# A graph attention layer on one core: the first stage rewritten, from the loading of x to the first row of weights

## The reference

```python
h = maximum(layernorm(x), 0.0)              # eps 1e-5
Wh = h @ W_w + W_b
e = leaky_relu((Wh @ a1)[:, None] + (Wh @ a2)[None, :], negative_slope=0.2)
attention = softmax(where(adj > 0, e, -9e15), axis=1)
out = x + attention @ Wh
```

## Time and profile before

| | us |
|---|---|
| median of 3 runs (lowest, highest) | 1554.79 (1554.2, 1555.71) |
| the profiled execution, its whole time | 1553.04 |
| the profiled execution, span from first to last instruction | 1551.1 |
| busy: PE, DVE, ACT, POOL | 1448.3, 1425.4, 1110.9, 593.7 |

### The profile page before, as it was taken

The page is one execution under the profiler, slowest core; times in us unless marked ns, Lnnn a source line. Parts: engine busy times, 40 slices in busy tenths (PEclk is TensorE's granted clock), DMA queues, the critical chain, the costliest instruction groups (busy, mean ns, idle before and its releaser), DMA issues.

```text
span 1551.1 us, 30326 instructions
## 1 busy us (share of the span) xinstructions
PE 1448.3 (93%) x12740; PEld 1258.0 (81%) x12740; DVE 1425.4 (92%) x1155; ACT 1110.9 (72%) x975; POOL 593.7 (38%) x1096
## 2 busy tenths in 40 slices
PE   2880899979999999999999999999999999999998
PEld 2760787768888888888888888888888888888887
DVE  4654999999999999999999999999999999999994
ACT  3664788877777677768777777768777777767771
POOL 0866433334444344334434343434343434423000
PEclk9995899999999999999999999999999999999999
DMA  9719866668776777778777877778767877676000
GB/s 195 80 14 118 65 44 48 44 60 103 56 55 59 100 56 52 52 84 81 52 52 63 100 54 53 60 99 57 54 49 62 103 55 53 49 97 50 1 1 28
DMA packets 170768, 99.07 MB, mean 64 GB/s; under 512 B 19472, under 2 KB 167568, under 8 KB 170640
## 3 DMA queue, kind: packets, MB, share of 16 engines
q0 software_dynamic: 147456, 67.17, 61.2%
q1 hardware_dynamic: 23184, 30.05, 7.1%
HBM read 290.06 MB, written 8.42 MB: 192 GB/s over the span
## 4 chain that ended last, share of the span: by engine, by line
PE 82%; DVE 12%; issue 2%; DMA 2%; ACT 1%; SPq 0%; DVEq 0%; POOL 0%; ACTq 0%; POOLq 0%
PE acc L636 77%; DVE work L515 4%; PE acc L612 3%; DVE work L508 3%; DVE X L521 1%; DMA work<-in_x 1%; PE acc L604 1%; DMA q_rows<-q_j 1%; DVE adj_cols L457 1%; DVE xr L408 1%; ACT work L323 1%; PE acc L647 0%; DMA work<-q_rows 0%; DVE xr L414 0%; ACT work L338 0%
## 5 line engine op out<-in xcount | busy, mean ns | idle before, releaser
L636 PE MATMUL acc<-X,work 128*128 128x257 f16 x12288 | 1372.6, 273 | 12.9 <-DVE work L515 12.9
L636 PEld LDWEIGHTS acc<-X,work 128*128 128x128 f16 x12288 | 1189.4, 97 | 188.8 <-DVE work L515 16.8
L251 POOL DMA_DIRECT2D adj_rows<-in_adj x1024 | 550.8, 545 | 776.0 <-DVE adj_cols L457 752.5
L338 ACT ACTIVATE work<-work 128x2048 f16<-128x2048 f32 x256 | 487.6, 1907 | 276.7 <-PE acc L636 274.0
L508 DVE SCALAR_TENSOR_TENSOR work<-work,sigma,adj_cols 128x2048 f32<-128x2048 f32 x256 | 594.6, 2323 | 20.8 <-issue 17.3
L515 DVE SCALAR_TENSOR_TENSOR work<-work 128x2048 f16<-128x2048 f32 x256 | 584.9, 2285 | 29.3 <-ACT work L338 29.2
L323 ACT ACTIVATE work<-work,r_j 128x1024 f32<-128x1024 f32 x256 | 278.1, 1134 | 28.3 <-DMA work<-q_rows 17.9
L323 ACT ACTIVATE work<-q_odd,r_j 128x1024 f32<-128x1024 f32 x256 | 278.5, 1135 | 23.3 <-DVE work L515 23.3
L457 DVE STREAM_TRANSPOSE adj_cols<-adj_rows 128x512 int32<-128x512 int32 x256 | 176.0, 699 | 0.0
L612 PE MATMUL acc<-q_odd,xr 128*128 128x258 f32 x256 | 68.8, 393 | 9.0 <-DVE X L426 9.0
L647 PE MATMUL acc<-mean_wh,tiny 128*128 128x257 f16 x64 | 17.7, 276 | 47.1 <-DVE work L515 46.5
(11 more groups left out here) (60 smaller groups left out, 54.0 us busy)
## 6 DMA issues: line engine op xcount, KB each, us to landing
adj_rows<-in_adj POOLq DMA_DIRECT2D x1024, 64.0 KB, 3.7
work<-in_x SPq DMA_DIRECT2D x16, 512.0 KB, 21.4
xr<-in_x SPq DMA_DIRECT2D x16, 512.0 KB, 4.0
out<-xr SPq DMA_DIRECT2D x16, 512.0 KB, 3.8
work<-q_rows SPq DMA_DIRECT2D x4, 512.0 KB, 5.7
q_odd<-q_rows SPq DMA_DIRECT2D x4, 512.0 KB, 5.4
q_odd<-in_L_gnn_W_w SPq DMA_DIRECT2D x2, 128.0 KB, 2.1
xr<-in_L_gnn_a SPq DMA_DIRECT2D x2, 128.0 KB, 6.1
```

What stands on the lines that cost most here:

```text
L251: pool.dma_start(rows8[QP * q:QP * (q + 1), n % R8], adj_v[s, m, k, q]).then_inc(s_rows[n % R8], 16)
L338: nc.scalar.mul(Et[:, at:at + 2, 0, :], Wt[:, i % RING], SCALE).then_inc(s_H, 1)
L636: return nc.tensor.matmul(acc[:, m, 0:F1], Et[:, 2 * (k % RING) + e, 1 if n == 2 else 0, m * P:(m + 1) * P], X16[:, 2 * k + e, 1 if n == 1 ...
```

## The change

- **x in seven groups** of 4, 4, 8, 8, 8, 16 and 16 blocks. The first group is issued ahead of W. The bias is no longer waited for at the start.
- **Norm factors on VectorE alone**: the inverse root by three Newton steps from a guess made from the exponent (in place of ACT's square root). The statistics of later groups are spread over the pairs by a table, so that all of them lie in pairs 0 to 18 of 32.
- **Blocks in pairs.** ACT normalises in place in x; POOL sums h in place of Wh. ACT copies the transposed even blocks, VectorE the odd ones. Six banks of PSUM hold h W (without bias), and the f16 parts of c_j h_j W are made straight from there: c_j is a factor of the pair's own t (`column_exps`, `greater_t`, `scale_columns`), so it needs no extremes. `x_high` on ACT and `x_low` on VectorE thus lie in the pair loop and no longer in the first super row; L426's addition is gone. r_j and sigma take up the pair's factor: sigma has a column for each unit.
- **Bias**: the softmax weights sum to one, so W_b is added to the rows of x that the output needs, by an accumulating DMA from POOL once per half super row.
- **Extremes over partitions** by a matmul against the identity, a maximum, and a matmul that spreads the two values.
- **q**: the eighth of q that the first super row needs is stored by a DMA of its own and loaded at once; the other stores follow. POOL holds further adjacency loads until it is there. The first 8 sets of adjacency are issued quadrant by quadrant between the additions.
- **First super row**: the first unit is multiplied alone, and ACT makes its upper part after two products in place of four.

```diff
+    GROUPS = [(0, 0, 1, 0), (0, 1, 2, 4), (0, 2, 4, 8), (1, 0, 2, Y), (1, 2, 4, Y + 8), (2, 0, 4, 2 * Y), (3, 0, 4, 3 * Y)]
+    STATS_AT = [None, None, (0, 2), (2, 2), (5, 2), (8, 4), (14, 4)]
...
             sp.wait_ge(s_qn, 1)
-            for q in range(NQ):
-                sp.dma_start(q_store[q], q_j[QP * q:QP * (q + 1), :].rearrange("p (z e) -> p z e", e=4)).then_inc(s_qst, 16)
+            store_q(0, 0, NZ // 2, s_q0)
+            sp.wait_ge(s_q0, 16)
+            load_q(0)
+            store_q(0, NZ // 2, NZ, s_qst)
+            for q in range(1, NQ):
+                store_q(q, 0, NZ, s_qst)
             sp.wait_ge(s_qst, 16 * NQ)
-            load_q(0)
+            sp.wait_ge(s_X, NB)
...
+            def add_bias(s, half):
+                pool.wait_ge(s_xr[half], 16 * s + 16)
+                pool.dma_start(xr[:, half], W_b.rearrange("(o m f) -> o m f", o=1, m=1).broadcast_to([P, H, F]),
+                               accum_op=ALU.add).then_inc(s_xb[half], 16)
+
+            for b in range(1, NB):
+                add_h(b)
+                if EARLY <= b < EARLY + NQ * SETS:
+                    load_quadrant(*divmod(b - EARLY, NQ))
+            pool.wait_ge(s_q, 16)
             for n in range(SETS, NSET * NS):
                 load_adj(n)
+                if n % NSET == 2 * R8 + 3:
+                    for half in range(2):
+                        add_bias(n // NSET, half)
...
+            for p in range(PAIRS + 1):
+                if p >= 2:
+                    x_high(2 * p - 4)
+                    x_high(2 * p - 3)
+                if 2 * p + 3 < NB:
+                    normalise(2 * p + 3)
+                if p >= 1:
+                    column_exps(p - 1)
+                if 2 * p + 2 < NB:
+                    copy_hT(2 * p + 2)
+                if 2 * p + 4 < NB:
+                    normalise(2 * p + 4)
...
+            def pair(p):
+
+                copy_hT(2 * p + 1)
+                if p >= 1:
+                    read_s_t(p - 1)
+                norms(p, 0)
+                if p >= 1:
+                    greater_t(p - 1)
+                norms(p, 1)
+                if p >= 2:
+                    x_low(2 * p - 4)
+                norms(p, 2)
+                if p >= 2:
+                    x_low(2 * p - 3)
+                norms(p, 3)
+                if p >= 1:
+                    scale_columns(p - 1)
...
-            def unit_low(g, i):
-                if g < NC:
-                    x_low(NI * g + i)
-                low(g, i)
...
+            def project(b):
+                k = b % 2
+                pe.wait_ge(s_hT[k], b // 2 + 1)
+                if b >= WH:
+                    pe.wait_ge(s_X, b - WH + 1)
```

More of the change, by code:

```diff
@@ L284, in copy_hT @@
+            def copy_hT(b):
                 act.wait_ge(s_ht, b + 1)
-                if not first:
+                if b >= 2:
                     act.wait_ge(s_whp, b - 1)
-                nc.scalar.copy(hT[:, k, :], ps_hT[k][:, 0:F]).then_inc(s_hT, 1)
-            normalise(0, 0, True)
-            normalise(1, 1, True)
-            copy_hT(0, 0, True)
-            normalise(2, 0, False)
-            copy_hT(1, 1, True)
-            def pairs(lo, hi):
-                with act.Fori(lo, hi) as pair:
-                    for k in range(2):
-                        normalise(2 * pair + k + 1, (k + 1) % 2, False)
-                        copy_hT(2 * pair + k, k, False)
@@ L301, in _ @@
[L301 to L312 removed]
+                nc.scalar.copy(hT[:, 0, :], ps_hT[0][:, 0:F]).then_inc(s_hT[0], 1)
@@ new lines, in _ @@
+            for p in range(PAIRS):
+                pair(p)
+                if p == 0:
+                    bounds()
+                if p >= PAIRS - TURNED:
+                    transpose(0, p - PAIRS + TURNED)
+            read_s_t(PAIRS - 1)
+            dve.wait_ge(s_st, PAIRS)
+            t_in = s_t[:, :, 1]
+            nc.vector.tensor_reduce(ext[:, 0:1], t_in, AX.X, ALU.max)
+            step(nc.vector.tensor_reduce(sc[:, 4:5], t_in, AX.X, ALU.min))
+            nc.vector.tensor_scalar(ext[:, 1:2], sc[:, 4:5], -1.0, None, ALU.mult).then_inc(s_ext, 1)
@@ L625, in _ @@
-            transpose_h(NB - 1, 1, False)
-            project(NB - 2, 0, False)
-            project(NB - 1, 1, False)
-            pe.wait_ge(s_sum, NB)
-            for k in range(2):
-                ins = nc.tensor.matmul(ps_tot[:, 0:F], ones, wh_sum[:, k, :], start=(k == 0), stop=(k == 1))
+            transpose_h(0)
+            transpose_h(1)
+            pe.wait_ge(s_wa, KF)
+            project(0)
+            transpose_h(2)
+            project(1)
+            pe.wait_ge(s_ones, 1)
+            pe.wait_ge(s_bound, 1)
@@ new lines, in _ @@
+            nc.tensor.matmul(ps_sum, ones, sc[:, 16:17], start=True, stop=True).then_inc(s_sq, 1)
+            for b in range(2, NB - 1):
+                transpose_h(b + 1)
+                if b == 5:
+                    pe.wait_ge(s_sqr, 1)
+                project(b)
+            project(NB - 1)
+            pe.wait_ge(s_ext, 1)
+            nc.tensor.matmul(ps_top[0:2, 0:P], ext[:, :], ident, start=True, stop=True).then_inc(s_extT, 1)
+            pe.wait_ge(s_dg, 1)
+            nc.tensor.matmul(ps_top[:, P:P + 2], ones[0:2, :], sc[0:2, 22:24], start=True, stop=True).then_inc(s_top, 1)
@@ L631, in _ @@
+            pe.wait_ge(s_hsum, NB - 1)
+            pe.wait_ge(s_X, NB - 3)
+            for c in range(KF):
+                ins = nc.tensor.matmul(ps_hb[:, c * P:(c + 1) * P], h_sum[:, c * P:(c + 1) * P], ones, start=True, stop=True)
+            ins.then_inc(s_col, 1)
+            pe.wait_ge(s_hb, 1)
+            for c in range(KF):
+                ins = nc.tensor.matmul(ps_mean[:, 0:F], hb[:, c * P:(c + 1) * P], Wx[:, c, 0:F], start=(c == 0), stop=(c == 1))
             ins.then_inc(s_tot, 1)
```

527 lines of the change are left out of this document (292 added, 235 removed).

## The result

The changed kernel takes **1511.35 us** (median of 4 runs, 1510.69 to 1512.79); the kernel before, run beside it, 1555.1 us. The ratio is 0.9718, with a 95% interval of 0.9704 to 0.9732: 43.8 us faster, where the prediction said 28.5 (1526.6). The time lies outside the central forecast (1519 to 1533) and 0.35 us inside the lower end of the wide range (1511 to 1546). That it is still inside is luck: one of the four runs, 1510.69, is not. So the direction and the course of the time line held, and the size was 15 us off. The profiled run took 1511.28 us with a span of 1509.5.

A forecast was written before the change was run, and what follows sets the result against it. VectorE was taken to bound the first row, and only time before 350.0 us could move. That row ending 28.2 us earlier gave a span of 1522.9; plus 1.94 and 1.75, 1526.6 us (central 1519 to 1533, wide 1511 to 1546).

The forecast's parts named there:

- Start: Before the pair loop: with x's first 4 blocks issued first, the loop starts at about 17 us instead of 27.
- Pairs 0 to 18: First part of the pair loop, bound by VectorE: its work and waits sum to 77 us, ending at 94 us.
- rival (a): VectorE's small steps in pairs 0 to 18 are cheaper and miss POOL's additions: 62 us there, 1511 in all; chance 0.15.
- port waits: In pairs 0 to 18, POOL's additions hold up small VectorE operations: 4 us over the pairs, 5 in five chains.
- Pairs 19 to 31: Rest of the pair loop: ACT sets the pace at 2.4 us a pair, 31 us, ending at 125 us.
- Rival (b): Something new (TensorE's clock in pairs 0 to 18, q, or adjacency) is late by 6 to 20 us; chance 0.23.
- Extremes: After the pair loop: two tiny matmuls and small steps replace POOL's 5.90 us; 5.5 to 6 us to q, at 131.
- q: q's way through DRAM before the first unit: store 3.0 us, load 4.4, back at 138.5 us.
- First unit: After q is back: products, weights and low part let TensorE start 9.1 us later, at 147.6 us.
- First row: TensorE becomes the bound, VectorE next by 0.29 us a unit; cold clock costs 3.4; 174.2 us, ending at 321.8.
- Edits that cost nothing: The bias by accumulating DMA from POOL after the row's 28th set, and sigma per pair, add no time.
- From span to median: Outside the kernel's span: 1.94 us around it, plus 1.75 by which the runs' median exceeded the profiled run.

The follow-up runs named there:

- the last kernel: The changed kernel with POOL's pause, copies of pairs 0 to 18 on ScalarE, four filled chain pairs and 48 extra matmuls before the first unit: 1503.76 us.

## Why the prediction was right in direction and short in size

**What bounds the kernel** was read rightly: only the time before 350.0 us moved. **Start**: 16.46 us for 17.

**Pairs 0 to 18** is the mis-sized term, 77 forecast and 69.66 measured. A statistics pair on VectorE (start, duration, what):

```profile
54.33 0.42 DVE L476 COPY xr<-acc 128x256 f32<-128x256 f32 x1
54.66 0.15 DVE L481 COPY xr<-acc 128x4 f32<-128x4 f32 x1
54.73 1.39 DVE L438 BATCH_NORM_STATS2 xr<-work 128x6 f32<-128x256 f32 x4
56.05 0.19 DVE L486 TENSOR_SCALAR xr<-xr 128x1 f32<-128x1 f32 x1
56.16 0.86 DVE L496 SCALAR_TENSOR_TENSOR X<-acc,c_j,X 128x256 f16<-128x256 f32 x2
56.94 0.21 DVE L492 TENSOR_SCALAR c_j<-c_j,sc 128x2 f32<-128x2 f32 x1
57.07 0.41 DVE L476 COPY xr<-acc 128x256 f32<-128x256 f32 x1
```

From start to start the copy takes 0.33 us, the read of s and t 0.07, the greater t 0.11, the two low parts 0.78 and the factors 0.13: 1.42 us instead of 1.78. The three small operations make 0.29 of the difference, the copy and the low parts the rest. I had priced the three at 0.2 each, the spacing of two that wait for one another; here none reads what the one ahead wrote, and each shows 0.15 to 0.21 us of duration but takes 0.07 to 0.13 of the engine's time. The difference of 0.36 in 19 pairs is 6.8 us. The port waits were 9 in the sum, 4 in the pairs and 5 in the chains; leaving the additions out shortens the chain pairs by 3.8 us and the whole stretch by 4.2 to 4.6, so about 4.6 was too much. Together 11.4 too much. Against it stand 3.2 us that I did not have, VectorE's waits up to pair 19 for TensorE's transposes (1.7), for the bound on W (1.1) and for an exponential (0.4). In one place the two overlap: 0.7 us of wait for transposes in pair 13 is also gone without the additions. So 0.9 to 1.6 us is left that I did not follow. The chains themselves were sized rightly: their dependent operations come 0.20 to 0.21 apart (62.54 to 62.75).

The mechanism of rival (a) is thus what happened in this term, with half of its 15 us; that its total, 1511, is also the measured one is luck, the sum of six smaller misses of the same sign.

**Pairs 19 to 31**: TensorE binds them, with 2.19 us a pair once the clock is up, not ScalarE with 2.4; the three pairs at reduced clock gave 1.25 us of that back.

**Rival (b), the clock.** The prediction named a clock at 0.5 within the loop as a sign that it would be wrong. The clock did fall there, to 0.67 on average between 28.8 and 38.5 us, 0.79 between 49 and 57, 0.66 between 65 and 70 and 0.72 between 86 and 92, behind the gaps of the chain pairs. The Trainium skill's page that the prediction cited for this rival (TensorE: Matmul & The Clock Gate) describes such an alternation, and the trace agrees that it occurs; what the rival had wrong is the price. It said 5 to 15 us; the kernel with filled gaps puts it at about 1.2 us in pairs 19 to 21 and 0.8 in pair 13, and at nothing that shows in the statistics pairs, because VectorE, not TensorE, is late there. The price is that of this kernel: with the copies on ScalarE, up to 4.4 us of VectorE's waits hang on the half clock. The row that I used against the rival did not bear on this loop. The length of a single gap does not tell the two apart: the loop before idled for 3.02 us up to 45.05 and 3.17 up to 66.00 and its clock stayed at 1.00, while the changed one idled for 1.73 and 1.31 us in pairs 12 and 13 and fell to 0.50 at 66 us. What decides is open. One more reading was loose: the block of 2.15 us (30.17 to 32.32) was taken as one at half clock, though the granted clock of that stretch is given as 1.00. The figure itself holds, since a block of the changed kernel takes 2.15 us too (31.50 to 33.65), at a granted clock of 0.50.

**Extremes**: 4.97 for 5.8. The parts that the prediction lists add up to 5.3, not 5.8; of the rest, the two dots and their sum took 1.0 us instead of 1.5 (116.71 to 117.71) and the matmul 0.4 instead of 0.6, while the 16 small steps, each waiting for another, took 3.5 instead of 3.2. **q**: the store 1.52 for 3.0. My 3.0 was chosen between 2.1 and 11.79 with no row of its own; the runs show that the quiet price is 1.5 (under the 2 us that the prediction quotes from the Trainium skill as the fixed part of any DMA) and that the hold is what buys it. The load came back in 3.95 for 4.4. **First unit**: 9.09 for 9.1, with transposes and low parts hidden as forecast.

**First row**: 172.56 for 174.2. I took the slow stretch of before, 6.8 us, at half loss, 3.4; the clock rose after 5.4, which is 2.7, and the row as I count it here, from the first unit on, lacks eight matmuls of the mean, 0.9 us. What I missed is how little is behind it: I left VectorE 0.29 us of slack per unit, 9 us a row. It was busy 173.65 of 174.10 us, because of what it does beside the units, and the last kernel shows it as the bound at 172.1 (of which 0.9 is the wait for adjacency).

**Edits that cost nothing**: the accumulating DMA of the bias costs POOL 1.6 us for each issue and lands after 10.2 to 29.4 us, and no wait in the first row or later is on it.

**From span to median**: the run that was profiled lay 1.75 us below the median of before; that I carried over. For the changed kernel the two agree within 0.1, so the 1.75 was scatter of one run, not a property of the kernel.

## What to carry to other kernels

Price a small VectorE operation by the distance from its start to the next one's start, in a row of the same kind: 0.07 to 0.13 us where nothing waits, 0.2 where each needs the one before. A small transfer on the critical path is worth a wait on the queue that would flood it: the way of q was 5.6 us with the hold and 12.3 without, and the changed kernel did not miss the loads that were held; kernels that reach the first row earlier waited 0.8 to 0.9 us for one of them. And before an engine's clock or a busy share is counted as a loss, ask which engine ends last in that stretch: filling TensorE's gaps brought something only where VectorE had slack, and the same half clock cost more once VectorE had been given less to do.

## What the runs showed of the hardware that I had not expected

- Small VectorE operations from SBUF to SBUF that run into a POOL addition end with it: 0.59, 0.77 and 0.79 us for operations that otherwise take 0.17, 0.18 and 0.23 (8 or 16 elements per partition in the chains, 2 in the column factors). One of a single element per partition, L486, did not: 0.2 us in each of nine meetings. Low parts, which read PSUM, the statistics and the aggregations kept their times beside the same additions.
- A later row with the upper part of x in place of the low one takes 169.8 us instead of 170.80, with the same matmuls; why is open.
- The moment at which the clock rises after the first unit's start differed between 3.2 and 5.4 us in kernels whose first row is the same. Where nothing else was late (5.4, 4.8, 3.2) the first row took 172.6, 172.3 and 171.5 us. That is half of the difference in time at half clock, and more than some edits were worth.
- Two profiles of one kernel differ by 0.7 us at pair 19 and 0.6 in the span, and four traces of the same loop by 1.9 us at pair 19, so single traces can't settle an edit smaller than that.
